# The delta stage of an eight-stage network: narrow sums in four column tiles, pieces of work split by engine, and a planner with weights by kind of piece

## The reference, cut to what matters

```python
q, k, v = (silu(causal_conv4(h @ w.T)) for w in (q_w, k_w, v_w))
beta = sigmoid(h @ b_w.T)
q, k = l2norm(q), l2norm(k)                 # per head, over 32 values
v, kb = v * beta, k * beta
A = strictly_lower(-kb @ k.T)               # 32 x 32 for each chunk and head
inv = (I - A) ** -1                         # row by row in the reference
u, w = inv @ v, inv @ kb
for c in chunks:                            # a state of 32 x 32 for each head
    attn = lower(q[c] @ k[c].T); ui = u[c] - w[c] @ S
    o[c] = q[c] @ S + attn @ ui; S = S + k[c].T @ ui
branches = fir3(v0), fir7(v0), fir15(v0), fir31(v0), v0, o     # v0 before beta
gate = softmax(mlp(h, mean(abs(branch)) over each head) / temperature)
out = (rmsnorm(sum(gate * branches)) * gain) @ o_w.T
```

## Time and profile before

| | |
|---|---|
| median of 3 runs | 4061.53 us |
| the profiled execution | 4069.63 us, span 4067.8 us |
| the delta stage in it | from 3007.5 to 3811.1 us |
| TensorE, VectorE, ScalarE, GpSimd over the whole span | 82%, 69%, 57%, 31% busy |

### The profile page before, as it was taken

How to read it: one execution, slowest core, us unless ns; L and a number is a source line. 1 busy time by engine, 2 the same in 40 slices (tenths; PEclk the granted TensorE clock), 3 DMA queues, 4 the chain that set the end, 5 groups by cost and what they waited for, 6 DMA issues and landing times. The chain is left out here.

```text
span 4067.8 us, 87613 instructions
## 1 busy us (share of the span) xinstructions
PE 3327.7 (82%) x36096; PEld 1530.1 (38%) x36096; DVE 2801.7 (69%) x4300; ACT 2313.1 (57%) x3864; POOL 1252.5 (31%) x1018
## 2 busy tenths in 40 slices
PE   5999999899657767799778888888976676766799
PEld 1222222366301112366433333333535555554444
DVE  8898899587599998887534677746435657656643
ACT  3888788666645554466421666656635454633464
POOL 1100000155358677455431010001004566651100
PEclk7999999999867877899899999988986586756799
DMA  4101010100011001100253021101000000000000
GB/s 99 27 9 28 21 21 1 36 1 1 15 26 30 17 16 32 32 2 1 43 76 43 9 42 35 33 16 39 1 13 3 4 4 4 3 4 2 30 1 21
DMA packets 138627, 85.51 MB, mean 21 GB/s; under 512 B 94770, under 2 KB 109892, under 8 KB 138100
## 3 DMA queue, kind: packets, MB, share of 16 engines
q1 hardware_dynamic: 135478, 75.64, 8.7%
q0 software_dynamic: 2688, 4.20, 0.7%
q10 hardware_dynamic: 64, 0.07, 0.0%
HBM read 47.90 MB, written 18.60 MB: 16 GB/s over the span
## 5 line engine op out<-in xcount | busy, mean ns | idle before, releaser
L948 DVE TENSOR_REDUCE attn_peak_halves<-attn_ps 128x2 f32<-128x1024 f32 x512 | 601.7, 1219 | 62.6 <-PE attn_ps L779 54.9
L901 ACT ACTIVATE attn_weights<-attn_ps 128x512 f32<-128x512 f32 x1024 | 530.9, 602 | 104.5 <-PE attn_ps L807 104.4
L3533 POOL TENSOR_TENSOR delta_q<-delta_q,delta_weighted 128x512 f32<-128x512 f32 x240 | 339.1, 1441 | 265.3 <-ACT delta_weighted L3917 265.3
L2902 DVE TENSOR_REDUCE sparse_peak<-sparse_ps 128x4 f32<-128x1024 f32 x256 | 309.3, 1223 | 134.9 <-PE sparse_ps L2532 133.2
L1204 POOL TENSOR_TENSOR moe_hidden<-moe_exact,moe_hidden 128x512 f16<-128x512 f32 x256 | 296.8, 1163 | 328.7 <-ACT moe_hidden L1188 320.1
L2762 ACT ACTIVATE sparse_weights<-sparse_ps 128x512 f32<-128x512 f32 (+1 forms) x512 | 272.0, 585 | 177.2 <-PE sparse_ps L2599 89.4
L245 PE MATMUL moe_ps<-moe_xT_halves,moe_w_halves 128*128 128x512 f16 x1536 | 363.9, 384 | 9.7 <-DVE moe_w_halves L1221 5.9
L807 PE MATMUL attn_ps<-attn_q_stack,attn_k_stack 50*128 50x512 f16 x1024 | 321.1, 385 | 35.0 <-DMA attn_q_stack<-attn_peak_rows 8.3
L1715 POOL TENSOR_TENSOR mamba_out_c<-mamba_states,mamba_c_rep 128x1024 f32<-128x1024 f32 x128 | 301.2, 2364 | 153.8 <-DVE mamba_states L1781 125.6
L245 PE MATMUL ffn_ps<-ffn_layers,ffn_h_halves 128*128 128x512 f16 x1536 | 334.4, 379 | 3.6 <-ACT ffn_gate L3131 3.6
L1505 PE MATMUL mamba_ps<-mamba_stack,mamba_spread 96*128 96x512 bf16 x512 | 196.6, 494 | 160.3 <-ACT mamba_decays L1669 83.6
(11 more groups left out here) (476 smaller groups left out, 6436.4 us busy)
## 6 DMA issues: line engine op xcount, KB each, us to landing
mamba_stack<-mamba_parts SPq DMA_DIRECT2D x96, 128.0 KB, 2.4
sparse_factor<-sp_factor SPq DMA_DIRECT2D x24, 256.0 KB, 3.7
sp_halves<-sparse_parts SPq DMA_DIRECT2D x8, 512.0 KB, 2.9
ffn_h<-in_h SPq DMA_DIRECT2D x4, 1024.0 KB, 8.0
attn_q_stack<-attn_halves SPq DMA_DIRECT2D x96, 32.0 KB
attn_k_stack<-attn_halves SPq DMA_DIRECT2D x96, 32.0 KB
attn_halves<-attn_hp SPq DMA_DIRECT2D x8, 384.0 KB, 3.3
attn_q_stack<-attn_peak_rows SPq DMA_DIRECT2D x128, 2.0 KB
```

Of the source, the lines that this page charges most:

```text
L901: act.activation(weights[:, at % 2, h, :], use.slot, ACT.Exp).then_inc(*key_act.one())
L948: dve.tensor_reduce(peak_halves[:, turn % PEAKS, keys, at:at + 2], use.slot, AX_X, ALU.max).then_inc(*score_dve.one())
L2902: dve.tensor_reduce(peak[:, at % PEAKS, unit // 2, 4 * r:4 * r + 4], use.slot.rearrange("p h (a k) -> p (h a) k", a=2), AX_X, ALU.max).the ...
L3533: pool.tensor_tensor(so_far, so_far, weighted[:, half, :], ALU.add).then_inc(*long_added.one())
```

## The change

It has three parts, all in the delta stage.

1. The sums of squares and the mean absolute values are made in four column tiles. For each 128 tokens t, a product with 32 stationary columns writes PSUM partitions 32t to 32t+31. A *stat* piece is four such products of 128 moving columns in place of one of 512. *sums* becomes 16 products with `sum_ones` as the stationary operand, which add up four rows of results for each tile; the root and the reciprocal then cover 128x128. *stat_end* becomes four activations of 32x128. `stats`, `w_stats` and `w_alpha` have 32 partitions in place of 128.
2. Pieces that had parts on several engines become pieces of one engine, in chains of their own: *raw* and *convolve*, *spread* and *lengthen*, *heads* and *turned*, *keep* and *kept*, *sources* and *token*, *absolute* and *stat*, *scaled* and *long_tap* (each half by itself). *silu* of v becomes a piece *values* of its own, behind the squares. The semaphores between the engines stay, apart from the wait for `silued` that moves to the first *absolute*.
3. The costs are written anew, the urgency becomes 0.004, and `AHEAD` moves single kinds of pieces forward or back in the choice.

```diff
-def planned(chains, needs, costs, urgency, tables, banks_for, frees, large=()):
+def planned(chains, needs, costs, urgency, ahead, tables, banks_for, frees, large=()):
...
-                possible.append((begin - urgency * to_end[piece], which, begin, piece, part, filled))
+                possible.append((begin - urgency * to_end[piece] - ahead.get(piece[0], 0.0), which, begin, piece, part, filled))
...
-    "raw": [("pe", 2.3), ("act", 1.1), ("dve", 4.0)], "beta": [("pe", 2.3), ("act", 1.2)], "silu": [("act", 5.2)],
-    "sums": [("pe", 5.8), ("act", 0.3), ("dve", 0.6)], "spread": [("pe", 2.7), ("act", 1.2)],
-    "scale": [("pool port", 4.6), ("dve port", 2.6)], "temper": [("act", 4.5), ("dve", 0.7)],
-    "heads": [("pe", 1.4), ("act", 1.7)], "cross": [("pe", 1.1), ("dve", 2.3)],
-    "level": [("pe", 0.9), ("dve", 0.45)], "grow": [("pe", 1.15), ("dve", 0.9)],
-    "uw": [("pe", 1.9), ("act", 0.8)], "keep": [("pe", 3.0), ("dve", 0.9), ("act", 0.45)],
-    "step": [("pe", 0.33), ("dve", 0.2)], "tap": [("dve port", 1.3)], "long_tap": [("act", 1.4), ("pool port", 2.6)],
-    "ruled": [("pe", 1.8), ("dve", 0.7)], "stat": [("act", 0.63), ("pe", 1.5)], "stat_end": [("act", 0.7)],
-    "hidden": [("pe", 4.2), ("act", 1.4)], "logits": [("pe", 2.8), ("dve", 0.9), ("act", 0.35)], "mix": [("dve", 1.4)],
-    "token": [("pe", 1.2), ("dve", 2.1)], "square": [("act", 0.65)], "root": [("dve", 0.7), ("act", 0.35)],
-    "o_scale": [("dve", 1.0)], "turn": [("pe", 0.8), ("act", 0.6)], "out": [("pe", 1.4), ("dve", 0.7)]}
+    "raw": [("pe", 3.0)], "convolve": [("act", 1.1), ("dve", 3.9)], "beta": [("pe", 2.6), ("act", 1.2)],
+    "silu": [("act", 4.2)], "values": [("act", 1.1)],
+    "sums": [("pe", 1.6), ("act", 0.35), ("dve", 0.95)], "spread": [("pe", 2.8)], "lengthen": [("act", 1.2)],
+    "scale": [("pool port", 4.8), ("dve port", 2.7)], "temper": [("act", 4.5), ("dve", 0.7)],
+    "heads": [("pe", 1.9)], "turned": [("act", 1.7)], "cross": [("pe", 1.15), ("dve", 2.4)],
+    "level": [("pe", 0.95), ("dve", 0.45)], "grow": [("pe", 1.0), ("dve", 0.9)],
+    "uw": [("pe", 1.9), ("act", 0.8)], "keep": [("pe", 3.6)], "kept": [("dve", 0.9), ("act", 0.45)],
+    "step": [("pe", 0.33), ("dve", 0.2)], "tap": [("dve port", 1.5)], "scaled": [("act", 0.72)], "long_tap": [("pool port", 1.44)],
+    "ruled": [("pe", 1.8), ("dve", 0.7)], "absolute": [("act", 0.63)], "stat": [("pe", 0.6)], "stat_end": [("act", 1.0)],
+    "hidden": [("pe", 3.8), ("act", 1.4)], "logits": [("pe", 3.3), ("dve", 0.9), ("act", 0.35)], "mix": [("dve", 1.4)],
+    "sources": [("pe", 1.6)], "token": [("dve", 2.65)], "square": [("act", 0.65)], "root": [("dve", 0.7), ("act", 0.35)],
+    "o_scale": [("dve", 1.0)], "turn": [("pe", 1.0), ("act", 0.6)], "out": [("pe", 1.8), ("dve", 0.7)]}
...
+DELTA_FILLED_BY = {"convolve": "raw", "lengthen": "spread", "turned": "heads", "kept": "keep", "token": "sources"}
+URGENCY = 0.004
+AHEAD = {"kept": 1.5, "root": 1.5, "sums": 0.5, "norm_root": 0.5, "uw": 0.5, "raw": 2, "hidden": 0.5, "temper": -2, "o_scale": -0.5,
+         "values": -0.5, "apply": -2, "silu": -1, "turned": -0.5, "mix": -0.5, "moments": -0.5}
...
-        chains.append([("raw", b, n) for n in RAW_ORDER] + [("silu", b), ("sums", b), ("spread", b, 1), ("spread", b, 0)])
+        chains.append([("raw", b, n) for n in RAW_ORDER])
+        chains.append([("convolve", b, n) for n in RAW_ORDER] + [("silu", b), ("sums", b), ("spread", b, 1), ("spread", b, 0)])
+        chains.append([("lengthen", b, 1), ("lengthen", b, 0)])
+        for n in RAW_ORDER:
+            needs["convolve", b, n] += [("raw", b, n)]
+        for n in range(2):
+            needs["lengthen", b, n] += [("spread", b, n)]
+        chains.append([("values", b)])
+        needs["values", b] += [("silu", b)]
...
-                chain += ([("heads", b, pair), ("cross", b, pair)]
+                chain += ([("cross", b, pair)]
...
+                chains += [[("heads", b, pair), ("turned", b, pair)], [("kept", b, pair)]]
+                of_way = ("keep",) + divmod(PAIRS * b + pair - 2, PAIRS)
+                needs["heads", b, pair] += [("scale", b)] + ([of_way] if b or pair > 1 else [])
+                needs["uw", b, pair] += [("turned", b, pair)]
+                needs["kept", b, pair] += [("keep", b, pair)]
...
-        long_taps = [("long_tap", b, k) for k in range(FIR_TAPS[LONG])]
-        needs[long_taps[0]] += [("scale", b)] + ([("long_tap", b - 1, FIR_TAPS[LONG] - 1)] if b else [])
-        chains += [taps, long_taps]
+        needs[taps[0]] += [("values", b)] + ([("sources", b - 1, 1, TPC - 1)] if b else [("features", CHUNKS - 1)])
+        scaled = [("scaled", b, k, half) for k in range(FIR_TAPS[LONG]) for half in range(HALVES)]
+        long_taps = [("long_tap",) + piece[1:] for piece in scaled if piece[2]]
+        needs[scaled[0]] += [("scale", b)] + ([("scaled", b - 1, FIR_TAPS[LONG] - 1, 1)] if b else [])
+        for _, _, k, half in scaled:
+            if k:
+                needs["long_tap", b, k, half] += [("scaled", b, k, half)]
+            if k > 1:
+                needs["scaled", b, k, half] += [("long_tap", b, k - 1, half)]
+            elif k and b:
+                needs["scaled", b, k, half] += [("long_tap", b - 1, FIR_TAPS[LONG] - 1, half)]
+        chains += [taps, scaled, long_taps]
...
+        chains.append([("absolute", b, half, i) for i in range(BRANCHES)])
+        for i in range(BRANCHES):
+            needs["stat", b, half, i] += [("absolute", b, half, i)]
+            if no or i > 1:
+                needs["absolute", b, half, i] += [("stat", b, half, i - 2) if i > 1 else ("stat",) + before + (BRANCHES - 2 + i,)]
...
+    return planned(chains, needs, PIECE_COST, URGENCY, AHEAD, TABLE, banks_for, frees, ("cross", "keep"))
...
-        stat_select = load("stat_select", [P, BRANCHES, P])
+        stat_select = load("stat_select", [P, BRANCHES, 32])
...
                 def sum_squares(b):
-                    use, first_of_head = one("sums", b), block_ones[:].rearrange("p (h d) -> p h d", h=KH)[:, :, 0]
+
+                    use = one("sums", b)
                     pe.wait_ge(*squared.at(b + 1))
                     wait_empty(use)
-                    for n in (1, 0):
-                        for t in range(TPB):
-                            at = (n * TPB + t) * KH
-                            made = pe.matmul(use.slot[:, at:at + KH], lengths[:, n, t * P:(t + 1) * P], first_of_head,
-                                             start=True, stop=True)
+                    for i, row in enumerate((2, 3, 0, 1)):
+                        n, half = row // HALVES, row % HALVES
+                        for t in range(TPC):
+                            at = half * BANK + t * P
+                            made = pe.matmul(use.slot[32 * t:32 * (t + 1), 0:P], sum_ones[:, row, :],
+                                             lengths[:, n, at:at + P], start=i == 0, stop=i == 2 * HALVES - 1)
                     made.then_inc(*wide_full.one())
...
-                                of_head = roots[:, 1, n, half * TPC + t, h:h + 1].broadcast_to([P, KD])
+                                row = 32 * t + KH * (HALVES * n + half) + h
+                                of_head = net.ident[:, row:row + 1].broadcast_to([P, KD])
                                 made = pe.matmul(use.slot[KD * h:KD * (h + 1), t * P:(t + 1) * P], of_head,
-                                                 net.ident[:], start=True, stop=True)
+                                                 roots[:], start=True, stop=True)
...
-                    pe.matmul(use.slot, stat_select[:, p, :], absolute[:, i % 2, :], start=i == 0,
-                              stop=i == BRANCHES - 1).then_inc(*stat_summed.one())
+                    for t in range(TPC):
+                        made = pe.matmul(use.slot[32 * t:32 * (t + 1), 0:P], stat_select[:, p, :],
+                                         absolute[:, i % 2, t * P:(t + 1) * P], start=i == 0, stop=i == BRANCHES - 1)
+                    made.then_inc(*stat_summed.one())
...
                 def silu(b):
-                    outs = (q_all[:, b % 3, :], k_all[:, b % 2, :], v_all[:, b % 3, HISTORY:])
+                    outs = (q_all[:, b % 3, :], k_all[:, b % 2, :])
                     act.wait_ge(*wide_dve.at(one("raw", b, RAW_ORDER[-1]).over))
-                    for n in (1, 0, 2):
+                    for n in (1, 0):
                         made = act.activation(outs[n], outs[n], ACT.Silu)
-                    made.then_inc(*silued.one())
-                    act.wait_ge(*silued.at(b + 1))
+                    settle(made)
                     if b:
                         act.wait_ge(*q_scaled.at(b))
                     for n in (1, 0):
                         made = act.activation(lengths[:, n, :], outs[n], ACT.Square)
                     made.then_inc(*squared.one())
 
+                def values(b):
+                    v = v_all[:, b % 3, HISTORY:]
```

(12 more changed lines are left out.)

144 lines of the change are left out of this document (76 added, 68 removed).

## The result

The changed kernel takes 4014.1 us (median of 4 runs, 4001.9 to 4015.3) where the kernel before takes 4059.1 (4052.3 to 4066.6): a ratio of 0.988, interval 0.9855 to 0.9909, or about 45 us less. The forecast was 89 us less. The profiled executions differ by 55.4 us (4069.6 and 4014.2), since that of before lies some 10 us above its median. Between them the delta stage alone went from 803.6 to 741.0, which is 62.6 us, while the unchanged stages ahead of it took 6.4 us more (it begins at 3013.9 and not at 3007.5). Of the runs further down, *split_long_taps* had two executions in which the granted clock was far lower (4519.9 and 8008.0 us at 0.69 and 0.57); they are left out of its time.

The account below looks back on a forecast made before the run. The delta stage's middle was taken as bound by the order of work and how full TensorE is kept. Front 17, middle 65 and tail 7 made 89 us less, 4061.5 to 3972 us; 8-in-10 range 3918 to 4046.

Parts of the forecast that it names:

- Sign and range: Whole kernel: faster, with a chance of 0.87, and 3918 to 4046 us for 8 in 10.
- third rival: Middle of the delta stage: TensorE's clock falls and takes back 35 us; about 4007 us, chance 0.08.
- The prediction's own test for a wrong cause: First cross product to last keep: at 590 us or more, TensorE did not set the middle's length.
- its signs of being right: Delta stage: convolutions within 12 us, sums 1.3 to 1.6, stat 0.3 to 0.6, middle 515 to 530, TensorE share near 71%.
- Front, projections, 9.9 us: First batch: raw in its own chain lets VectorE's three convolutions run back to back, 9.9 us less, all on the path.
- Front, lengths, 5.6 us: First batch's sums: 16 narrow products take 1.34 us where sums took 6.99, so 5.6 us go.
- Middle, work: Middle: stat at 0.45 us saves 29 us, three sums 17; TensorE's work falls from 433 to 387 us.
- the other rule weighed: Column tiles in the delta stage: changing tiling mode drains TensorE, costing at most 21 us, or nothing added.
- Middle, share: Middle: TensorE stays at its old 71.5% busy share, so 387 us of work take 541 us, 65 less.
- The second rival: Middle: VectorE's queue sets the pairs' chain, TensorE's freed time turns idle, only fixed parts come; about 4035 us, chance 0.17.
- Tail, 7 us: After the last keep: five shorter stat pieces save 7.9 us, stat_end costs 0.5 more, 7 us less.
- Slower rival: Middle: short taps and long taps' additions overlap and slow each other; half the stops give 4080 us, chance 0.08.

Follow-up runs that it names:

- split_long_taps: Kernel before with one split alone, each long tap's scaled copies and additions planned as pieces for one half: 4042.6 us, ratio 0.9947.
- old_order_tiles: Kernel before, its order kept, with only the column tiles of the change for lengths and means: 4059.9 us, ratio 0.9996.
- old_order_stat: Kernel before with only the means in column tiles, lengths as before: 4069.6 us, ratio 1.0021.
- old_times_new_pieces: Changed kernel, its pieces and column tiles kept, planned by the durations of the kernel before, urgency 0.003 and no weights: 4083.7 us, ratio 1.0044.
- joined_long_taps: Changed kernel with each long tap's scaled copies and additions one piece of the plan again, cross products also waiting for scaled values: 4095.9 us, ratio 1.0089.
- new_order_wide: Changed kernel with its order kept, lengths and means computed by the old wide products: 4014.0 us, ratio 0.9884.

## Why the prediction was half right

**Sign and range** held: 4014 lies in 3918 to 4046. The sum was twice too large, and its middle had the wrong cause, so that the range held is in part luck: the order gave some of what TensorE's relief was to give. The nearest single number was the third rival's, 4007 with a chance of 0.08. The prediction's own test for a wrong cause was a middle of 590 us or more; it was 584, and needed the experiments to tell. Of its signs of being right, the convolutions (within 11.6 us) and the share (0.72) came true. The others were missed, some narrowly: *sums* took 1.94 us (1.3 to 1.6), a *stat* 0.63 and all 48 of them 30.2 (0.3 to 0.6, below 30), and the last keep came 585 us after the first cross product (515 to 530).

**Front, projections, 9.9 us:** right. From the stage's start the last of the three convolutions ends 10.2 us sooner (36.3 and 26.1 us). **Front, lengths, 5.6 us:** the size was near (*sums* 1.94 us for 1.34), the claim that all of it is on the path was not. In the old order 1.5 us came through to *spread*; in the new one 3.8 reached the first cross product and none the whole time. The step that I left out is who takes the result next and what stands ahead of it in that queue. What the front gained besides comes from the order of VectorE's queue: in the kernel before, the second batch's third convolution, that of v (3084.9 to 3088.8), stood ahead of the first cross product; now the cross product comes 1.3 us behind that of q, which ended at 3073.6.

**Middle, work:** a *stat* of 0.63 us was inside the bounds and above the 0.45 taken. But "TensorE then has 387 us to do" failed in another way, and by more: it had 421. With the means and lengths narrow, the clock in the middle was lower (0.67 for 0.71 in the same order), and the gate's products gave 23.5 us back. The Trainium skill (TensorE: Matmul & The Clock Gate, What's actually happening) has the direction: throttled unless activity releases it. That is the third rival's mechanism. In the new order it alone is enough for the tiles to bring nothing, since 6.5 us of TensorE's time were left. That the rest was not on the path either is what *old_order_tiles* says, where 17 us in the middle brought at most 7, if nothing else in that edit took them back. Of the other rule weighed, that a change of tiling mode drains the engine (TensorEngine Tiling (Array Packing), Key Properties), no run separates a price.

**Middle, share:** this is the step that failed. I took the middle as TensorE's work over 71.5%, and after the change that reading even fits (0.72). But the share doesn't hold from kernel to kernel: *old_order_stat* keeps it at 0.72 (427.2 of 597.2), *old_order_tiles* has it at 0.70 (416.1 of 594.8), *old_times_new_pieces* at 0.69, *joined_long_taps* at 0.66 and *new_order_wide* at 0.73. For 421 us of work that would be a middle anywhere from 579 to 633. The work isn't fixed either, as the same products took 39 us less of TensorE's stage in the new order. The second rival had this right, that relief of TensorE turns to idle time, and wrong that the order moves nothing.

**Tail, 7 us:** a *stat* there took 0.65 us where it took 2.08, but the time shows nothing of it (*old_order_stat*, 1.0021). The 20 us that did come are the ring's, which starts its last round sooner. I had cut the stage at the last keep and taken that for what the tail waits for; it waits for the last taps.

**Slower rival:** taps and additions do slow each other (additions half as wide shorten VectorE's busy time by 31 us, taps half as wide GpSimd's by 15), but the median tap stayed at 1.29 us.

Open stay: which of durations and urgency *old_times_new_pieces* lost by (both were set back); why one order beats another beyond what the table shows; how much of the tiles' small net relief *stat_end* and the wider root took back; and whether the 105 to 113 us of the last round can be shortened.

## What to carry to other kernels

A high busy share of one engine is no proof that its work sets the time: give that engine less to do with the order held fixed, check in the trace that its busy time did fall, and see. Where a planner writes the order, any edit to its pieces or durations is a new draw, here worth from 1.2% less to 1.2% more for the same work, so measure edit and order apart before either gets the credit. And follow the result of a shortened product to its taker's place in its queue before counting a microsecond.

## What the hardware showed that was not expected

Making the means and lengths in narrow column tiles lowered the granted clock of a stretch from 0.71 to 0.67 in the same order, and the gate's 512-column products behind the means went from 612 and 592 ns in the mean to 847 and 826: the narrower products saved 50 us of TensorE's time and 6.5 remained. The old order shows the same: 0.69 to 0.67, 672 and 630 ns to 885 and 888, and 20.6 us left of 60.

The order alone moved the clock too. The same products took 548.3 us of TensorE in one order of the stage (granted clock 0.67) and 509.6 in another (0.71).

GpSimd's additions over half as many columns took 134 us off GpSimd in the middle and 31 off VectorE, whose own instructions had not been changed (the 100 short taps of the stage went from 144 to 127 us).
